# First layer of all tiles ahead of the feed-forward, low-rank term as a matrix per batch, gate once for all

## The chip, the cores and the metric

The kernel runs on one core of a Trainium2 chip. The metric is the device time of one execution in microseconds (us), as the median of several runs. The core has TensorE (matmul), VectorE, ScalarE and GpSimd, each with its own instruction queue in program order, and SyncE (SP), which here only issues transfers. Engines meet only at semaphores.

## The reference, cut to what matters

There are B = 32 batches of L = 128 tokens with D = 128 channels, R = 16 columns of `fside`, E = 4 experts and H = 512 hidden channels.

```python
# layer 0: linear + low-rank term made from fside, exact gelu, residual
z1 = einsum('bfi,bir->bfr', x, F) / 128          # F = fside[:, 0], 128 x 16 per batch
z  = einsum('bfr,bor->bfo', z1, F) / 16
x  = x + gelu_exact(x @ W.T + fc_bias + z + cond[:, None, :])

# layer 1: gate on means of token segments, top 2 of 4 experts, plus a shared one
gate_in = concat(mean(all), mean(head, proprio), mean(wrist, proprio))
logits  = (gate_in @ gate_w + gate_b) * (1 + scale) + shift   # scale, shift from silu(cond) @ time_w + time_b
w_be    = top-2 of softmax(logits), renormalised
for e in range(4):                                # expert 1 leaves out the wrist tokens, expert 2 the head tokens
    out += w_be[:, e] * mask[e] * (gelu_tanh(x @ ew1[e] + eb1[e]) @ ew2[e] + eb2[e])
x = x + out + gelu_tanh(x @ sw1 + sb1) @ sw2 + sb2
```

## The kernel before

Activations lie transposed, channels on the 128 partitions and tokens along the free dimension. A tile is NB = 4 batches, so TOK = 512 columns; there are NT = 8 tiles. Every product but transposes and small sums is done as three fp32r matmuls (`product3`, L541 to L546): each operand is split into a high half (rounded to fp32r) and a low half (the rest), and hi\*hi, lo\*hi and hi\*lo are added up in PSUM. So each weight and each activation needs a high and a low half, made by ScalarE, VectorE or GpSimd.

A feed-forward step is a pair (tile t, expert s), s = 0 being the shared one. `up(t, s)` on TensorE gives four chunks of 128 hidden channels in a ring of UP = 5 PSUM banks. `gelu` on ScalarE reads them into `h` (L468), for s = 0 a second time into `hs_hi` (L470). `split` on VectorE multiplies `h` by the routing weight into `hs_hi` (L864) and `hs_lo` (L872), four batches each; for expert 4 the high half is ScalarE's (`expert4_high`, L452), and the shared low half is GpSimd's (`shared_low`, L371). `down` on TensorE adds the second product of all five steps up in one bank. Experts 2 and 3 (s = 2, 3) work on 344 of the 512 columns. Then VectorE adds the residual (`outT`, L901), TensorE transposes, ScalarE copies, SP stores.

The loop runs over tiles, two in a pass. Inside the steps of tile t stands, in small pieces, the first layer of tile t + 1: transposing `x` (`xT`, L564), its two halves, the low-rank input product with `F` (`low_rank_in`), a mask to keep each batch to its own 16 rows (`z1_mask`, L754), the halves of `z1` and `fT` (`fT_low`, L762 and L764), `layer0` (L541 to L598) with five products, the exact gelu (`gelu0`, L437, with a table switch at L442), `residual0` (L771 to L775), the segment sums and the gate of four batches (`gate_in`, `gate_logits`, `gate_weights`, L782 to L838). Loads are issued by SP two tiles ahead. GpSimd adds the output biases into `x1` (L362). All order is written out by hand: each engine's program is a fixed list with semaphore waits.

Of the kernel before, what the change touches and what calls it, by code (L numbers as in the profile page):

```python
# [6 lines left out]
F32R = mybir.dt.float32r  # L19
# [5 lines left out]
def build(nc, x, fside, cond, W, fc_bias, gate_w, gate_b, time_w, time_b,  # L25
# [14 lines left out]

    NS = E + 1
    SPAN = [(0, L), (0, L), (0, HEAD + PROP), (HEAD, L), (0, L)]
    Z_SCALE = 1.0 / (D * R)
    ZR = NB * R
    BIAS_HI, BIAS_LO = ZR, ZR + 32
    UP = 5
    BANK_Y, BANK_OUT, BANK_L0 = 5, 6, 7


    GATE_LINKS = 14  # L50

    with ExitStack() as ctx:
# [8 lines left out]

        x_tok = sb("x_tok", [128, 2, NB, D])
        F_raw = sb("F_raw", [128, 2, 2, ZR])
        W_raw = sb("W_raw", [128, D])
        cond_raw = sb("cond_raw", [B, D])

        cond_rows = sb("cond_rows", [128, 2, D])
# [13 lines left out]
        batch_rows = sb("batch_rows", [128, NB])  # L81
        zmask_halves = sb("zmask_halves", [128, 2, NB])
        zmask = sb("zmask", [128, NB])
        before = sb("before", [128, NB, E, E])

        WT_hi = sb("WT_hi", [128, D], F32R)
        WT_lo = sb("WT_lo", [128, D], F32R)
# [40 lines left out]
        equal = sb("equal", [128, NB, E, E])
# [873 lines left out]
```

## Time and profile before

| | us |
|---|---|
| median of 3 runs | 275.53 |
| lowest, highest | 274.08, 276.33 |
| span of the profiled execution | 274.8 |
| busy: TensorE, VectorE, ScalarE, GpSimd | 243.5, 242.8, 190.5, 86.3 |
| one tile in the loop (151.0 to 181.8) | 30.8 |

The span is that of one execution under the profiler, from the first to the last instruction. Busy time is the time in which an engine has an instruction at work. Matmuls are pipelined: one is still in flight when the next two have started, so their price is the distance between starts, not their length.

### The profile page before, as it was taken

The numbers are of one execution on the slowest core, as the hardware profiler recorded it, in microseconds if no ns is written. First come the engines' busy times: TensorE is split into PE (matmuls) and PEld (weight loads), VectorE is DVE, ScalarE is ACT, GpSimd is POOL, SyncE is SP. The second block draws the span as 40 slices with busy tenths as digits, with TensorE's granted clock in tenths as the row PEclk, the third lists the DMA queues.
The fourth block names the chain that finished last, engine by engine and source line by source line (L and its number), as shares of the span: only waits on it lengthen the run. The fifth ranks groups of instructions, "written<-read, shape, count | busy, mean of one in ns | idle before, by whom it ended". The sixth has DMA issues, their size and how long they took to land.

```text
span 274.8 us, 4417 instructions
## 1 busy us (share of the span) xinstructions
PE 243.5 (89%) x1235; PEld 206.0 (75%) x1235; DVE 242.8 (88%) x582; ACT 190.5 (69%) x331; POOL 86.3 (31%) x99
## 2 busy tenths in 40 slices
PE   8849929999889988999889988999889988999995
PEld 8637818987678767987678767987678767988884
DVE  2995999989997999989998999989997999999863
ACT  3936823996489856896489846896489856895361
POOL 7449503063301513062301513062302523070200
PEclk9977977999999999999999999999999999999999
DMA  4950000002100030002000030002000010001001
GB/s 118 327 98 2 1 0 1 0 2 75 15 2 0 0 87 0 0 0 76 10 0 0 0 87 0 0 0 78 9 0 0 0 41 2 0 0 38 2 0 38
DMA packets 20340, 7.63 MB, mean 28 GB/s; under 512 B 10644, under 2 KB 19048, under 8 KB 20328
## 3 DMA queue, kind: packets, MB, share of 16 engines
q1 hardware_dynamic: 19309, 7.28, 10.4%
q10 hardware_dynamic: 859, 0.19, 0.3%
q8 instruction: 5, 0.08, 0.1%
q0 software_dynamic: 160, 0.02, 0.1%
q14 instruction: 7, 0.06, 0.1%
HBM read 5.39 MB, written 2.10 MB: 27 GB/s over the span
## 4 chain that ended last, share of the span: by engine, by line
DVE 45%; PE 36%; issue 15%; ACT 2%; DVEq 1%; POOL 0%; POOLq 0%
PE ps L541 12%; PE ps L546 11%; PE ps L542 11%; DVE hs_lo L872 11%; DVE hs_hi L864 6%; DVE fT_bias L762 4%; DVE equal L813 3%; DVE outT L901 2%; DVE W_lo L242 2%; DVE z L754 2%; DVE logit L804 2%; PE ps L557 2%; DVE F_hi L745 1%; ACT h L468 1%; DVE equal L815 1%
## 5 line engine op out<-in xcount | busy, mean ns | idle before, releaser
L468 ACT ACTIVATE h<-ps,b_col 128x512 f32<-128x512 f32 (+1 forms) x160 | 97.1, 632 | 53.0 <-PE ps L546 52.9
L541 PE MATMUL ps<-hs_hi,W_hi 128*128 128x512 f32 (+3 forms) x180 | 65.9, 366 | 17.2 <-DVE hs_lo L872 17.1
L872 DVE SCALAR_TENSOR_TENSOR hs_lo<-h,w_be,hs_hi 128x512 fp32r<-128x512 f32 (+1 forms) x128 | 76.3, 657 | 2.7 <-ACT hs_hi L452 2.7
L371 POOL TENSOR_TENSOR hs_lo<-h,hs_hi 128x512 fp32r<-128x512 f32 x32 | 40.4, 1294 | 91.9 <-ACT hs_hi L470 91.9
L542 PE MATMUL ps<-hs_hi,W_lo 128*128 128x512 f32 (+3 forms) x180 | 63.1, 351 | 0.0
L546 PE MATMUL ps<-hs_lo,W_hi 128*128 128x512 f32 (+3 forms) x180 | 63.1, 350 | 0.0
L541 PE MATMUL ps<-x_hi,W_hi 128*128 128x512 f32 (+1 forms) x160 | 59.5, 372 | 3.9 <-DVE x_hi L773 3.9
L546 PE MATMUL ps<-x_lo,W_hi 128*128 128x512 f32 (+1 forms) x160 | 59.3, 371 | 0.5 <-DVE x_lo L775 0.5
L542 PE MATMUL ps<-x_hi,W_lo 128*128 128x512 f32 (+1 forms) x160 | 59.2, 370 | 0.0
L541 PEld LDWEIGHTS ps<-hs_hi,W_hi 128*128 128x128 f32 x180 | 34.4, 191 | 26.0 <-DVE hs_lo L872 22.7
L864 DVE TENSOR_SCALAR hs_hi<-h,w_be 128x344 fp32r<-128x344 f32 (+1 forms) x97 | 43.1, 505 | 4.6 <-ACT h L468 3.5
L546 PEld LDWEIGHTS ps<-hs_lo,W_hi 128*128 128x128 f32 x180 | 34.3, 191 | 4.0
L542 PEld LDWEIGHTS ps<-hs_hi,W_lo 128*128 128x128 f32 x180 | 34.4, 191 | 3.3
L541 PEld LDWEIGHTS ps<-x_hi,W_hi 128*128 128x128 f32 x160 | 30.5, 191 | 8.1 <-issue 4.0
L546 PEld LDWEIGHTS ps<-x_lo,W_hi 128*128 128x128 f32 x160 | 30.7, 192 | 5.3 <-DVE x_lo L775 1.2
L542 PEld LDWEIGHTS ps<-x_hi,W_lo 128*128 128x128 f32 x160 | 30.6, 191 | 4.1
L470 ACT ACTIVATE hs_hi<-ps,b_col 128x512 fp32r<-128x512 f32 x32 | 22.2, 693 | 0.0
L354 POOL TENSOR_TENSOR z_lo<-z,z_hi 64x512 fp32r<-64x512 f32 x7 | 9.0, 1284 | 37.9 <-ACT z_hi L433 37.9
L452 ACT ACTIVATE hs_hi<-h,w_be 128x512 fp32r<-128x512 f32 x31 | 19.9, 711 | 0.4
L349 POOL TENSOR_TENSOR xT_lo<-x,xT_hi 128x512 fp32r<-128x512 f32 x7 | 9.7, 1387 | 23.3 <-ACT xT_hi L422 23.3
L362 POOL TENSOR_TENSOR x<-x,bias 128x168 f32<-128x168 f32 (+1 forms) x24 | 11.2, 491 | 8.4 <-DVE bias L849 8.4
L242 POOL TENSOR_TENSOR W_lo<-W_raw,W_hi 128x512 fp32r<-128x512 f32 x7 | 10.9, 1568 | 8.2 <-DVE W_hi L236 4.1
(134 smaller groups left out, 289.6 us busy)
## 6 DMA issues: line engine op xcount, KB each, us to landing
W_raw<-in_L_cond_ew SPq DMA_DIRECT2D x8, 256.0 KB, 4.6
out<-out_tok SPq DMA_DIRECT2D x7, 256.0 KB, 2.2
x_tok<-in_x SPq DMA_DIRECT2D x16, 84.0 KB
x_tok<-in_x SPq DMA_DIRECT2D x7, 88.0 KB
W_raw<-in_L_cond_sw SPq DMA_DIRECT2D x2, 256.0 KB, 4.0
F_raw<-in_fside_Bx1x1024x SPq DMA_DIRECT2D x15, 32.0 KB, 2.1
cond_rows<-in_cond SPq DMA_DIRECT2D x16, 2.0 KB
out<-out_tok SPq DMA_DIRECT2D x2, 128.0 KB, 1.8
```

The costliest lines, as they stand in the source:

```text
L242: eng.tensor_tensor(lo, raw, f32(hi), ALU.subtract).then_inc(w_lo_ok[n], 1)
L362: nc.gpsimd.tensor_tensor(xb[:, :, at:at + n], xb[:, :, at:at + n], bias2[:, i, :].unsqueeze(2).to_broadcast([128, NB, n]), ALU.add).then_ ...
L371: nc.gpsimd.tensor_tensor(hs_lo[:, hf, c, :], h[:, hf, c, :], f32(hs_hi[:, hf, c, :]), ALU.subtract).then_inc(shared_lo_ok, 1)
L452: nc.scalar.activation(hs_hi[:, hf, :, c], h[:, hf, :, c], ACT.Copy, scale=w_be[:, b, E - 1:E]).then_inc(hi4_ok, 1)
L468: ins = nc.scalar.activation(dst, up_bank(s, c), ACT.Gelu_apprx_tanh, bias=b1_col[:, s, c:c + 1])
L470: ins = nc.scalar.activation(hs_hi[:, hf, c, :], up_bank(s, c), ACT.Gelu_apprx_tanh, bias=b1_col[:, s, c:c + 1])
L541: nc.tensor.matmul(dst, w_hi, m_hi, start=start, stop=False)
L542: nc.tensor.matmul(dst, w_lo, m_hi, start=False, stop=False)
L546: return nc.tensor.matmul(dst, w_hi, m_lo, start=False, stop=stop)
L762: nc.vector.tensor_tensor(fT_bias[lo_rows, :], cond_rows[lo_rows, par, :], f32(fT_bias[lo_rows, :]), ALU.subtract).then_inc(fT_lo_ok, 1)
L864: nc.vector.tensor_scalar(hs_hi[:, hf, :, c], h[:, hf, :, c], w_be[:, b, s - 1:s], None, ALU.mult).then_inc(hi_ok, 1)
L872: nc.vector.scalar_tensor_tensor(hs_lo[:, hf, :, c], h[:, hf, :, c], w_be[:, b, s - 1:s], f32(hs_hi[:, hf, :, c]), ALU.mult, ALU.subtract) ...
```

## The change

Everything is unrolled in Python; there is no loop instruction left. The work is in three stages:

- **First layer of all tiles.** `x1` and its halves have room for all 8 tiles. The low-rank term is folded into the weight: per batch `F F^T` is made by one fp32 matmul from the transposed `F` (`matrices`), VectorE scales it and adds `W^T` (`matrix`, the tile `mat`), and one fp32 matmul per batch gives the layer (`layer0`). So no halves, no mask, no `z1`. `fc_bias + cond` is one bias column per batch (`bias0`), and `gelu0` is four ScalarE instructions of 128 columns a tile.
- **The gate once.** The segment sums are taken two tiles at a time, the gate of all 32 batches in one sequence. It stands between the splits of the first three steps.
- **The feed-forward as a list of 40 steps** (`STEPS`): (0,0), (1,0), then for each tile its experts 1 to 4 followed by the shared step of tile t + 2. TensorE does `up(k + 2)`, `down(k)`. `h` has three buffers. VectorE now makes the high half of expert 4 and the shared low half (two instructions of 1024 columns); GpSimd only adds the 24 bias pieces after the gate. All low halves of weights are VectorE's (`weight_low`), all high halves ScalarE's (`weight_high`).

Loads: `x` and `fside` come in four chunks of 1, 1, 2 and 4 tiles (`CHUNKS`), all issued at the start; `fside` is loaded once and not twice.

```diff
-    UP = 5
+    CHUNKS = [(0, 1), (1, 2), (2, 4), (4, 8)]
+    STEPS = [(0, 0), (1, 0)]
+    for t in range(NT):
+        STEPS += [(t, s) for s in range(1, NS)]
+        if t + 2 < NT:
+            STEPS.append((t + 2, 0))
+    RING = [0, 1, 4, 2, 3]
+    UP = len(RING)
...
+            load_x(0, SEGS[:2])
+            load_F(1)
+            load_x(1)
+            load_F(2)
+            load_x(2)
+            load_weight(0)
+            load_weight(1)
+            load_F(3)
+            load_x(3)
...
+            pool.wait_ge(bias2_ok, 1)
+            for t in range(NT):
+                xb = x1[:, t, :].rearrange("p (b l) -> p b l", l=L)
...
+            def gelu0(t):
+                act.wait_ge(y_ps, t + 1)
+                if t >= 2:
+                    act.wait_ge(x1_ok, t - 1)
+                for b in range(NB):
+                    ins = nc.scalar.activation(g0[:, t % 2, b * L:(b + 1) * L], psY0[t % 2][:, b * L:(b + 1) * L],
+                                               ACT.Gelu, bias=bias0[:, t * NB + b:t * NB + b + 1])
+                ins.then_inc(g0_ok, 1)
+            def gelu(k):
+                t, s = STEPS[k]
+                if k == 2:
+                    act.wait_ge(x1_ok, NT)
+                if k >= 3:
+                    act.wait_ge(lo_ok, parts_until(k - 3))
+                if s == 0 and k >= 2:
+                    act.wait_ge(down_ok, k - 1)
...
+            for t in range(NT):
+                if t + 2 < NT:
+                    xT_copy(t + 2)
+                    fT_copy(t + 2)
+                gelu0(t)
+                if t in (3, 4):
+                    weight_high(t - 3)
+            act.wait_ge(b1_in, 32)
+            weight_high(2)
+            gelu(0)
+            gate_tanh()
+            weight_high(3)
+            gelu(1)
+            for n in range(4, 2 * NS):
+                weight_high(n)
+            for k in range(2, K):
+                gelu(k)
+                t, s = STEPS[k - 3] if k >= 3 else (0, 0)
+                if s == NS - 1:
+                    out_copy(t)
...
+            def matrices(t):
+                pe.wait_ge(fT_ok, t + 1)
+                if t >= 2:
+                    pe.wait_ge(M_ok, t - 1)
+                for b in range(NB):
+                    last = nc.tensor.matmul(psM[t % 2][:, b * D:(b + 1) * D], fT[:, t % 2, b, :], fT[:, t % 2, b, :],
+                                            start=True, stop=True)
+                last.then_inc(M_ps, 1)
...
+            for t in range(NT):
+                if t + 1 < NT:
+                    matrices(t + 1)
+                if t + 2 < NT:
+                    xT(t + 2)
+                    transpose_F(t + 2)
+                layer0(t)
+                if t == 3:
+                    pe.wait_ge(bias_in, 16 * 3)
+                    pe.wait_ge(silu_ok, 1)
+                    nc.tensor.transpose(psEb2T, eb2_raw[:, :], ident[0:E, 0:E]).then_inc(eb2T_ps, 1)
+                if t == 4:
+                    pe.wait_ge(eb2T_read, NSEG)
+                    pe.wait_ge(mod_terms_ok, 1)
+                    nc.tensor.matmul(psMod, ones[:, :], mod_terms[:, :, :], start=True, stop=True
+                                     ).then_inc(mod_ps, 1)
+            up(0)
+            pe.wait_ge(mod_read, 1)
+            pe.wait_ge(gate_fold_ok, 1)
+            nc.tensor.matmul(psLogit, ones[:, :], gate_fold[:, :, :], start=True, stop=True).then_inc(logit_ps, 1)
+            up(1)
+            for k in range(K):
+                if k + 2 < K:
+                    up(k + 2)
+                down(k)
+                t, s = STEPS[k - 1] if k >= 1 else (0, 0)
+                if s == NS - 1:
...
+                    out_transpose(t)
...
+            for t in range(NT):
+                if t + 1 < NT:
+                    matrix(t + 1)
+                residual(t)
+                if t == 2:
+                    time_gate()
+                if t == 4:
+                    output_rows()
+                if t == 5:
+                    dve.wait_ge(bias_in, 16 * 3)
+                    modulation()
+                halves(t)
+                if t % 2 == 1:
+                    segment_sums(t - 1, t + 1)
+                if t in (4, 5):
+                    weight_low(t - 4)
+            gate_in()
+            weight_low(2)
+            split(0)
+            gate_logits()
+            weight_low(3)
+            split(1)
+            gate_weights()
+            split(2)
+            output_biases()
+            for n in range(4, 2 * NS):
+                weight_low(n)
+            for k in range(3, K):
+                t, s = STEPS[k - 2]
+                if s == NS - 1:
+                    out_sum(t)
+                split(k)
+            out_sum(NT - 1)
```

In `up(k)`, TensorE waits for `w_lo_ok` (the low half of its weight) for tile 0's steps, and for `h_ok` of the chunk that had the bank five chunks before. In `split(k)`, VectorE waits for `h_ok` of all four chunks and for `down(k - 2)`. `residual`, `halves` and `matrix` are the VectorE steps of one tile of the first layer, `eb2T_read` is counted by `output_rows`.

## Rows read from the trace of the kernel before

**Rows 1.** The page: busy times, chain that ended last, rate of transfers, stores.
```profile
PE 243.5 (89%) x1235; PEld 206.0 (75%) x1235; DVE 242.8 (88%) x582; ACT 190.5 (69%) x331; POOL 86.3 (31%) x99
GB/s 118 327 98 2 1 0 1 0 2 75 15 2 0 0 87 0 0 0 76 10 0 0 0 87 0 0 0 78 9 0 0 0 41 2 0 0 38 2 0 38
...
DVE 45%; PE 36%; issue 15%; ACT 2%; DVEq 1%; POOL 0%; POOLq 0%
...
out<-out_tok SPq DMA_DIRECT2D x7, 256.0 KB, 2.2
```

**Rows 2.** Stretches: length, busy (count) by engine, granted clock, DMA share, GB/s.
```profile
40.00:45.00 5.00, 4.58 (x12) 3.68 (x13) 4.83 (x12) 0.63 (x1) 2.61 (x4) 0.57 0.00 0
151.00:181.80 30.80, 28.13 (x140) 23.51 (x140) 28.50 (x70) 22.91 (x40) 8.82 (x10) 1.00 0.08 19
```

**Rows 3.** Groups by line and shape: count, busy us, mean ns, idle before.
```profile
L371 POOL TENSOR_TENSOR hs_lo<-h,hs_hi 128x512 fp32r<-128x512 f32 x32 | 40.4, 1294 | 91.9 <-ACT hs_hi L470 91.9
...
L442 ACT ACT_TABLE_LOAD x8 | 10.3, 1283 | 2.6 <-issue 2.5
```

**Rows 4.** Timeline of one tile in the loop: start, length, engine, line.
```profile
150.88 0.69 ACT L468 ACTIVATE h<-ps,b_col 128x512 f32<-128x512 f32 x1
151.04 0.40 PE L542 MATMUL ps<-hs_hi,W_lo 128*128 128x512 f32 x1
...
152.01 0.71 ACT L468 ACTIVATE h<-ps,b_col 128x512 f32<-128x512 f32 x1
...
152.91 0.40 PE L541 MATMUL ps<-x_hi,W_hi 128*128 128x512 f32 x1
...
155.41 0.39 PE L546 MATMUL ps<-x_lo,W_hi 128*128 128x512 f32 x1
...
159.03 2.59 DVE L864 TENSOR_SCALAR hs_hi<-h,w_be 128x512 fp32r<-128x512 f32 x4 [0.31 <-issue]
...
160.21 0.32 PE L541 MATMUL ps<-x_hi,W_hi 128*128 128x344 f32 x1
...
161.97 0.32 PE L546 MATMUL ps<-x_lo,W_hi 128*128 128x344 f32 x1
```

**Rows 5.** Timeline of the first 51 us, same columns.
```profile
1.07 3.36 PE L557 MATMUL ps<-ones 128*128 128x128 f32 x14 [1.07 <-POOL ones L316]
4.38 1.09 PE L564 MATMUL ps<-ident,x_tok 128*128 128x128 f32 x4
...
10.02 3.94 DVE L242 TENSOR_TENSOR W_lo<-W_raw,W_hi 128x512 fp32r<-128x512 f32 x2
...
27.02 1.72 PE L557 MATMUL ps<-ones 128*128 128x128 f32 x14
...
27.75 0.17 DVE L804 TENSOR_TENSOR logit<-logit,gate_add 128x16 f32<-128x16 f32 x1
...
28.49 1.13 ACT L415 ACTIVATE W_hi<-W_raw 128x512 fp32r<-128x512 f32 x1
28.58 0.60 PE L564 MATMUL ps<-ident,x_tok 128*128 128x128 f32 x4
...
29.16 1.08 DVE L242 TENSOR_TENSOR W_lo<-W_raw,W_hi 128x512 fp32r<-128x512 f32 x1
...
31.80 0.63 ACT L415 ACTIVATE W_hi<-W_raw 128x512 fp32r<-128x512 f32 x1
...
36.04 1.68 DVE L864 TENSOR_SCALAR hs_hi<-h,w_be 128x512 fp32r<-128x512 f32 x4
...
37.63 2.74 DVE L872 SCALAR_TENSOR_TENSOR hs_lo<-h,w_be,hs_hi 128x512 fp32r<-128x512 f32 x4
...
40.42 0.79 PE L541 MATMUL ps<-hs_hi,W_hi 128*128 128x512 f32 x1 [4.19 <-DVE hs_lo L872]
...
47.77 1.32 DVE L864 TENSOR_SCALAR hs_hi<-h,w_be 128x344 fp32r<-128x344 f32 x4 [0.38 <-ACT h L468]
...
49.01 2.03 DVE L872 SCALAR_TENSOR_TENSOR hs_lo<-h,w_be,hs_hi 128x344 fp32r<-128x344 f32 x4
```

More of the change, by code:

```diff
@@ L198, in build @@
+        psOut = ps[:, 7, :]
         block = ctx.enter_context(nc.Block())
@@ L201, in f32, with chunk_of @@
             return ap.bitcast(F32)
+        def chunk_of(t):
+            return next(c for c, (a, z) in enumerate(CHUNKS) if a <= t < z)
         def span(ap, s):
@@ L444, in expert4_high @@
-            def expert4_high(t, par, first=0):
-                act.wait_ge(w_ok, t + 1)
-                act.wait_ge(h_ok, CH * (NS * t + NS))
-                for b in range(first, NB):
-                    c = slice(b * L, (b + 1) * L)
-                    hf = half(par, NS - 1)
-                    nc.scalar.activation(hs_hi[:, hf, :, c], h[:, hf, :, c], ACT.Copy, scale=w_be[:, b, E - 1:E]
-                                         ).then_inc(hi4_ok, 1)
-            def gate_tanh(t):
-                act.wait_ge(logit_x_ok, t + 1)
-                nc.scalar.activation(tanh_g[:, :, :], logit_x[:, :, :], ACT.Tanh, scale=0.5).then_inc(tanh_g_ok, 1)
@@ L529, in _, with gate_tanh, out_copy @@
-            gelu(0, 0, 1)
-            weight_high(9)
-            with act.Fori(0, NT - 3, 2) as t:
-                tile(t, 0)
-                tile(t + 1, 1)
-            tile(NT - 2, 0)
-            tile(NT - 1, 1, last=True)
+            def gate_tanh():
+                act.wait_ge(logit_x_ok, 1)
+                nc.scalar.activation(tanh_g[:, :, :], logit_x[:, :, :], ACT.Tanh, scale=0.5).then_inc(tanh_g_ok, 1)
+            def out_copy(t):
+                act.wait_ge(out_ps, t + 1)
+                nc.scalar.activation(x_tok[:, t, :, :], psOut.rearrange("p (b d) -> p b d", d=D), ACT.Copy
+                                     ).then_inc(out_tok_ok, 1)
@@ new lines, in down @@
+            def down(k):
+                t, s = STEPS[k]
+                if t == 0:
+                    pe.wait_ge(w_lo_ok, 2 * s + 2)
+                if s == 0 and t >= 2:
+                    pe.wait_ge(outT_ok, NSEG * (t - 1))
+                elif s == 0 and t == 1:
+                    pe.wait_ge(M_ok, NT)
+                    pe.wait_ge(fT_ok, NT)
+                pe.wait_ge(lo_ok, parts_until(k))
+                for c in range(CH):
+                    last = product3(span(psY[t % 2], s), W2_hi[:, s, c, :], W2_lo[:, s, c, :],
+                                    span(hs_hi[:, k % 2, c, :], s), span(hs_lo[:, k % 2, c, :], s),
+                                    s == 0 and c == 0, s == NS - 1 and c == CH - 1)
+                last.then_inc(down_ok, 1)
@@ L970, in _ @@
[L970 to L977 removed]
+            dve.wait_ge(WT_ok, 1)
+            matrix(0)
+            dve.wait_ge(condT_ps, 1)
+            nc.vector.tensor_copy(condT[:, :], psCondT).then_inc(condT_ok, 1)
+            dve.wait_ge(fcb_in, 16)
```

913 lines of the change are left out of this document (305 added, 608 removed).

## The prediction

> **What bounds the kernel now.** I read four views. The page's engine totals and chain come first [rows 1]: TensorE 89% and VectorE 88% busy, the chain of work that ended last split between VectorE (45%), TensorE (36%) and 15% of waits without a named cause. The reader should see two engines taking turns. The table by stretches [rows 2] shows one tile of the loop: 30.8 us, TensorE busy 28.1 at the full clock, VectorE 28.5. The groups [rows 3] show who makes the shared low half today: GpSimd, 32 of 1294 ns. ScalarE scales the fourth expert's high half. The timelines [rows 4, 5] give unit prices, always from start to start, since matmul ends overlap.
>
> TensorE: eight steps from 151.04 to 152.91 are 0.234 us for a 512-column matmul of `down`; 11 steps from 152.91 to 155.41 are 0.227 in `up`; 11 from 160.21 to 161.97 are 0.160 at 344 columns [rows 4]. A 128-column plain fp32 matmul stands as two passes: (1.72 - 0.15)/13 = 0.12 a pass; a transpose is (0.60 - 0.2)/3 = 0.13 [rows 5]. So 60 products of `up` and 60 of `down` cost 36 x 0.227 + 36 x 0.234 + 48 x 0.160 = 24.3 us a tile, and four output transposes 0.5: 24.8. The other 6 us of today's 30.8 are first-layer work and waits.
>
> **The stream afterwards.** All first-layer, gate and GpSimd work leaves the loop. TensorE keeps 24.8 us a tile. VectorE takes over the fourth expert's high half and the shared low half. With GpSimd idle its prices are the free ones [rows 5]: four 512-column scalings 1.68 us (2.59 in a tile where GpSimd runs [rows 4]), four of the low half 2.74, at 344 columns 1.32 and 2.03. Experts: 2 x 4.4 + 2 x 3.35 = 15.5. The shared half, two of 1024 columns, is not shown; between the 1.08 of a strided 512-column subtraction [rows 5] and 1.3 (half of the 2.74 for 4 x 512), I take 1.16 each: 2.3. Output sum 0.8. Total 18.6 us, under 24.8. ScalarE: 0.57 us per 512-column gelu (two in 152.01 - 150.88 [rows 4]), 0.46 at 344: 16 x 0.57 + 8 x 0.46 + 0.5 = 13.3. TensorE should bound.
>
> But one stall is new. `gelu` of a shared step k now waits for `down` of k-2 (`down_ok`), since it writes `hs_hi[k % 2]`; `down(k-2)` comes behind `up(k)`. Queued behind that gelu is everything of ScalarE, and TensorE's next `up(k+1)` waits for its `h_ok` through the ring of five banks. Counted from the end of `down(k-2)`: the first shared chunk is released after 2 x 0.57 + 0.2 = 1.35, the third after 3.65. `up(k+1)` writes chunk 0 at once, may write chunk 1 at 1.35 and chunk 3 only at 3.65, where without waiting it would start at 3 x 0.68 = 2.05. The difference, 1.6, with the handovers 1.8, is lost once per shared step from tile 2 on, six times: 10.8 us. A tile then takes 24.8 + 1.8 = 26.6 against 30.8 now.
>
> **The opening.** Tile 0's `x` is there at 4.4 [rows 5]. TensorE does 8 transposes (cold, 0.22 each), W's, the first matrices (8 passes, 1.0), tile 1's transposes, then after ScalarE's two copies `matrices(1)`, tile 2's transposes and `layer0(0)`: 12.9. Four gelus, and `residual(0)` starts at 14.0. Each tile costs TensorE 16 x 0.12 + 8 x 0.13 = 3.0 us and VectorE 3.1: `matrix` 0.67 (a two-input product of 512 columns is 2.74/4 [rows 5]), residual 0.62 and low half 0.68 (the same kind, estimated), high half 0.48 (a scaling, 1.68/4, and its handover), sums 0.67 (estimate, three reduces for two tiles at 0.45). Up to `residual(7)` that is 7 x 3.1 = 21.8. VectorE also does `time_gate` 1.6, `output_rows` 0.5, `modulation` 1.4 and two low halves of weights, 1.1 + 0.65: 5.2 in all (small operations at 0.2 [rows 5], 128 columns at 0.3 to 0.45). The two queues also hold each other up. TensorE's `mod` matmul waits for `eb2T_read`, which VectorE gives after `residual(4)`; behind it stand `matrices(6)`, `xT(7)` and `layer0(5)`. It idles 3.7 us, VectorE then 3.4 before `residual(5)` and 1.3 before `residual(7)`: 4.7 on the path. 14.0 + 21.8 + 5.2 + 4.7 = 45.7. Loads I cost at nothing: `xT(4)`, the first to need the last chunk, stands at 16.8, and `x`, `fside` and two weights, 2.9 MB, take 9 us at the 327 GB/s of the page's best slice [rows 1]. Without that cover each us later is a us of the path.
>
> **The gate, once.** It must end before `split(2)`, the first with a routing weight, and VectorE, ScalarE take turns. From 45.7: `gelu0(7)` is just done; `weight_high(2)` 1.1 (1.13 and 0.63 for the two kinds [rows 5]), table load 1.3 [rows 3], eight gelus 4.6: 52.7. `split(0)` 2.3: 55.0. Four operations up to `logit_x` 1.2, tanh 0.25, `weight_high(3)` 0.6, eight gelus: 61.7. Then ScalarE has `weight_high(4)` to (9), 3 x 1.08 + 3 x 0.56 = 4.9, in front of `gelu(2)`: 66.7, which is done at 69.0. `split(2)` 4.4: 73.5. Output biases 1.6 and `weight_low(4)` 1.1: 76.2. Only then may `up(3)` start. In these 31 us TensorE did three `up` and one `down`; it stands for 10.6 us before `up(3)`. In the kernel before, the wait for the first routed half was 4.2 us, ending at 40.42 [rows 5].
>
> After such an idle the clock is low: the stretch 40 to 45 us shows a granted 0.57 [rows 2], so 1.2 GHz up to about 44.3, roughly 4 us after the restart. I take 5 us, 2.3 lost.
>
> **The sum.** 76.3; eight tiles 198.2, less three `up` (8.2) and one `down` (2.8): 187.2; cold clock 2.3; six stalls 10.8; `down(39)` waits for its own split, which nothing follows, 2.9; output sum, copy, handovers and the store's 2.2 [rows 1]: 4.2. Together 283.7 us of span. The profiled execution of before is 274.8, its median 275.5, so I add 0.7: **284 us**, 3% slower. Put as a difference: 4.2 x 7 = 29 us gained in the stream, about 36 lost ahead of it, the rest at the end (the halves of the last tile are gone).
>
> Unknown prices. GpSimd adds all 24 bias pieces (11 us) just as VectorE makes `weight_low(4)` to (9). A low half stands at 2.0 under such contention and 1.08 without [rows 5]: 0.9 before `up(3)`, the others hidden behind `down(1)` and `up(4)`. From 0 to 2; I take 0. Tanh after Gelu early on may need its table: of the 1.28 us load [rows 3] two would cost ScalarE 2.6 and the path 0.8; I take none. The Trainium skill, "ScalarE: Activation LUTs", Table sets, lists tanh with exp and sigmoid and Gelu in another set: by it the sum is 284.5; no row here shows the pair.
>
> **Rivals.**
> *Cold opening.* TensorE has pauses in the opening; at 1.2 GHz a tile costs it 16 x 0.24 + 8 x 0.22 = 5.6 us, it bounds, and `residual(7)` moves by 11: 295. For it: 0.24 a pass is what the first 14 take [rows 5]. Against it: two thirds of its work there are plain matmuls, and it is busy 3.0 of 3.1 us. The Trainium skill, "TensorE: Matmul & The Clock Gate", Part 4, says that transposes do not count as activity; by that rule this case is likelier, and a third of the opening's work is transposes. Chance 0.1.
> *Not slower: ScalarE's shared gelu holds nobody up.* It would, if its start came 1.8 us earlier against `up(k+1)`, that is if `down(k-2)` of 344 columns ended before `up(k)` was through. The stream then takes 24.8 a tile: 284 - 10.8 = 273, within 1% or just past it. It decides from 6 us saved. Against it is the order of the queue: `down(k-2)` stands behind `up(k)`. Chance 0.1.
> *VectorE or ScalarE bound in the stream.* If the scalings stay near the 2.59 of today [rows 4] or a gelu takes 0.69 (its own length [rows 4]) from start to start, 288 to 291. Chance 0.15.
> *Shorter opening.* If the `mod` hold-up does not form and TensorE stays warm: 284 - 4.7 - 1.3 = 278. Chance 0.1. With the stall gone as well it would be below 272. All remaining chance, 0.55, is my forecast's.
>
> Here 1% is about what a measurement can tell from no change: 272.8 to 278.3 is the same. Slower 0.75 (forecast nearly whole, cold opening, other engines), same 0.17 (no stall, short opening), faster 0.08 (both). Range 275 to 293: it leaves out the colder half of the cold case and most of the no-stall case.
>
> **What would show it.** A start of `up(3)` near 76 with TensorE idle some 10 us before; a tile of 26.6 us with TensorE at full clock; a wait of about 1.8 us inside the `up` behind each shared step, released by ScalarE; VectorE near 70% and ScalarE near 50% in the loop. If `up(3)` starts before 68, or the loop's tile is under 25.3, I am wrong.

## The result

The changed kernel takes 287.5 us (median of 4 runs, 286.5 to 289.3) against 274.9 (274.1 to 276.3) of the kernel before: ratio 1.044, 95% interval 1.039 to 1.049, so 4.4% slower. The profiled execution has a span of 287.6 us, against 274.8 before. Ratios here and below leave disturbed executions out, so a ratio is not always the quotient of the two medians.

The page of the changed kernel answers to [rows 1]: busy times, then two of the rows by 40 slices (7.2 us each; tenths of busy time, tenths of full clock), then the chain that ended last.

```profile
span 287.6 us, 3352 instructions
PE 248.7 (86%) x1205; PEld 209.1 (73%) x1205; DVE 194.9 (68%) x395; ACT 142.9 (50%) x264; POOL 19.8 (7%) x39
...
PE   7889678554199999989998999899899989999964
...
PEclk9899755968579999999999999999999999999989
...
PE 67%; ACT 14%; DVE 8%; SPq 4%; issue 3%; DMA 2%; DVEq 0%; ACTq 0%
```

VectorE fell from 88% to 68% and GpSimd from 31% to 7%. The chain now belongs to TensorE for 67%, with ScalarE second. The slices show where TensorE rests (the 5, 5, 4, 1 of slices 8 to 11, about 50 to 79 us) and where its clock was down (slices 5 to 7 and 9 to 12).

**The loop.** The table by stretches, as [rows 2], with the stretch's length, busy time and count by engine, granted clock, DMA share and GB/s:

```profile
103.00:129.70 26.70, 25.57 (x125) 21.43 (x125) 18.19 (x37) 14.20 (x26) 0.00 (x0) 1.00 0.04 11
129.70:156.30 26.60, 25.53 (x124) 21.38 (x124) 18.19 (x37) 14.11 (x26) 0.00 (x0) 1.00 0.04 11
```

The chain passes the same matmul at 103.03, 129.68, 156.33, 182.99, 209.64 and 236.29 us: a tile is 26.65 us, against 30.80 before. VectorE needs 18.2 of it and ScalarE 14.2.

**The opening and the gate stage.** The residuals of tiles 0, 1, 5 and 7 (L533), what TensorE waited for in between, and the restart, from the timeline (start, length, engine, line, count, idle time before it and who ended it), which answers to [rows 5]:

```profile
11.30 0.82 PE L383 MATMUL ps<-ident,x_tok 128*128 128x128 f32 x4 [0.88 <-DMA x_tok<-in_x]
...
12.76 1.92 PE L409 MATMUL ps<-x,h 128*128 128x128 f32 x8
...
15.88 0.69 DVE L533 TENSOR_TENSOR x<-x,h 128x512 f32<-128x512 f32 x1 [4.74 <-ACT h L304]
...
19.09 0.69 DVE L533 TENSOR_TENSOR x<-x,h 128x512 f32<-128x512 f32 x1 [0.73 <-ACT h L304]
...
20.02 0.66 PE L383 MATMUL ps<-ident,x_tok 128*128 128x128 f32 x4 [1.06 <-DMA x_tok<-in_x]
...
31.38 0.70 PE L489 MATMUL ps<-mod_terms,ones 128*128 128x256 f32 x2 [3.26 <-DVE eb2T L608]
...
38.80 0.69 DVE L533 TENSOR_TENSOR x<-x,h 128x512 f32<-128x512 f32 x1 [4.08 <-ACT h L304]
...
47.73 0.69 DVE L533 TENSOR_TENSOR x<-x,h 128x512 f32<-128x512 f32 x1 [1.58 <-ACT h L304]
...
54.81 2.36 DVE L561 TENSOR_TENSOR hs_lo<-h,hs_hi 128x1024 fp32r<-128x1024 f32 x2 [1.74 <-ACT hs_hi L321]
...
58.38 0.31 ACT L327 ACTIVATE tanh_g<-logit_x 128x128 f32<-128x128 f32 x1 [3.60 <-DVE logit_x L638]
...
63.67 4.81 ACT L286 ACTIVATE W_hi<-W_raw 128x512 fp32r<-128x512 f32 x6
...
76.60 1.89 DVE L551 TENSOR_TENSOR W_lo<-W_raw,W_hi 128x512 fp32r<-128x512 f32 x2
...
77.72 0.66 PE L370 MATMUL ps<-x_hi,W_hi 128*128 128x344 f32 x1 [9.52 <-DVE W_lo L551]
```

`residual(7)` starts at 47.7 and `up(3)` at 77.7, after TensorE stood for 9.5 us. Before, TensorE's wait for the first routed half ended at 40.42 [rows 5]. So that restart comes 37.3 us later, and what is behind it takes 209.9 us where it took 234.4: 24.5 us shorter. The difference, 12.8 us, is the whole difference of the two spans.

### The profile page after: what moved, and what is told of

It reads as the page before. It is cut to its first block, busy times and chain, and to the rows that moved or that the text cites. A ratio compares the mean times of both kernels' runs of the same rounds, so it can differ in the third digit from the quotient of the medians.

```text
span 287.6 us, 3352 instructions
## 1 busy us (share of the span) xinstructions
PE 248.7 (86%) x1205; PEld 209.1 (73%) x1205; DVE 194.9 (68%) x395; ACT 142.9 (50%) x264; POOL 19.8 (7%) x39
## 4 chain that ended last, share of the span: by engine, by line
PE 67%; ACT 14%; DVE 8%; SPq 4%; issue 3%; DMA 2%; DVEq 0%; ACTq 0%
PE ps L370 20%; PE ps L372 20%; PE ps L371 19%; ACT h L318 6%; ACT hs_hi L321 4%; SPq L198 3%; PE ps L409 3%; DVE hs_lo L572 3%; DMA x_tok<-in_x 2%; ACT W_hi L286 2%; PE ps L399 2%; DVE hs_hi L567 2%; PE ps L458 1%; DVE hs_lo L561 1%; PE ps L383 1%
## 5 line engine op out<-in xcount | busy, mean ns | idle before, releaser
L572 DVE SCALAR_TENSOR_TENSOR hs_lo<-h,w_be,hs_hi 128x512 fp32r<-128x512 f32 (+1 forms) x128 | 77.3, 665 | 0.0
L567 DVE TENSOR_SCALAR hs_hi<-h,w_be 128x512 fp32r<-128x512 f32 (+1 forms) x128 | 49.4, 448 | 26.3 <-PE ps L372 25.0
L370 PE MATMUL ps<-hs_hi,W_hi 128*128 128x512 f32 (+1 forms) x160 | 60.2, 376 | 2.5 <-DVE hs_lo L572 2.5
L372 PE MATMUL ps<-hs_lo,W_hi 128*128 128x512 f32 (+1 forms) x160 | 59.5, 372 | 0.0
L371 PE MATMUL ps<-hs_hi,W_lo 128*128 128x512 f32 (+1 forms) x160 | 59.3, 371 | 0.0
L561 DVE TENSOR_TENSOR hs_lo<-h,hs_hi 128x1024 fp32r<-128x1024 f32 x16 | 18.9, 1221 | 33.2 <-ACT hs_hi L321 33.2
L271 POOL TENSOR_TENSOR x<-x,bias 128x168 f32<-128x168 f32 (+1 forms) x24 | 15.7, 691 | 71.6 <-DVE bias L675 71.6
L331 ACT ACTIVATE x_tok<-ps 128x512 f32<-128x512 f32 x8 | 4.8, 599 | 30.3 <-PE ps L458 30.3
L409 PE MATMUL ps<-x,h 128*128 128x128 f32 x64 | 12.2, 353 | 2.9 <-issue 2.9
L304 ACT ACTIVATE h<-ps,bias 128x128 f32<-128x128 f32 x32 | 9.1, 367 | 9.7 <-PE ps L409 9.7
L409 PEld LDWEIGHTS ps<-x,h 128*128 128x128 f32 x64 | 11.1, 261 | 3.6 <-issue 3.4
```

The source lines that it names most:

```text
L271: nc.gpsimd.tensor_tensor(xb[:, :, at:at + n], xb[:, :, at:at + n], bias2[:, i, t * NB:(t + 1) * NB].unsqueeze(2).to_broadcast([128, NB, n ...
L304: ins = nc.scalar.activation(g0[:, t % 2, b * L:(b + 1) * L], psY0[t % 2][:, b * L:(b + 1) * L], ACT.Gelu, bias=bias0[:, t * NB + b:t * NB ...
L370: nc.tensor.matmul(dst, w_hi, m_hi, start=start, stop=False)
L371: nc.tensor.matmul(dst, w_lo, m_hi, start=False, stop=False)
L372: return nc.tensor.matmul(dst, w_hi, m_lo, start=False, stop=stop)
L409: last = nc.tensor.matmul(psY0[t % 2][:, b * L:(b + 1) * L], mat[:, t % 2, b, :], x1[:, t, b * L:(b + 1) * L], start=True, stop=True)
```

## The experiments

The kernels below are the changed kernel with the edit shown; nothing is left out of the computation in any. "Idle matmuls" are 128-column fp32 products of ones into a PSUM bank that nothing reads before it is overwritten; they only keep TensorE busy. The times, and three numbers from each one's profile that tell the runs apart (starts in us, and the time from `up(3)` to the end):

| kernel | median us | ratio to before | residual(7) | up(3) | up(3) to end |
|---|---|---|---|---|---|
| changed kernel | 287.5 | 1.044 | 47.7 | 77.7 | 209.9 |
| e_swap | 278.1 | 1.011 | 47.6 | 77.5 | 196.9 |
| e_modlate | 284.7 | 1.031 | 45.0 | 75.0 | 208.0 |
| e_warmmod | 286.5 | 1.041 | 45.9 | 75.9 | 207.9 |
| e_warmopen2 | 290.9 | 1.045 | 50.7 | 80.6 | 210.0 |
| e_warmgate | 288.2 | 1.044 | 50.2 | 80.2 | 205.9 |
| e_gatefirst2 | 285.9 | 1.036 | 48.5 | 74.7 | 210.2 |
| e_high | 288.7 | 1.046 | 49.9 | 77.3 | 208.0 |
| e_pool | 281.2 | 1.021 | 49.2 | 67.7 | 209.8 |

Each ratio's interval is 0.4 to 0.8% to either side. The kernel before took 274.9 us beside the changed kernel and 276.1 to 276.5 beside the others, so ratios compare whole times better than medians do: 1% is 2.8 us. The opening also differs from execution to execution: in the profiles of the eight kernels other than e_warmopen2, none of whose edits acts before it, `residual(1)` starts anywhere from 19.1 to 22.8 us. So stages are compared below from one point of the profile to the next; each is read in one execution.

### 1. The stall in the loop

`down(k)` is put ahead of `up(k+2)` where that one is of a shared step, so that the shared gelu finds `down_ok` done:

```diff
+                early = k + 2 < K and STEPS[k + 2][1] == 0
+                if early:
+                    down(k)
                 ...
-                down(k)
+                if not early:
+                    down(k)
```

> TensorE's queue only: where the step after next is a shared one, down(k) is issued before up(k + 2), so ScalarE's shared gelu can start 1.9 us earlier against the following up. My theory (the wait for down(k-2) behind up(k) holds ScalarE and through the ring TensorE): the 1.8 us wait inside six ups is gone, a tile takes 24.8 us and not 26.65, the whole 10 to 11 us less (about 277). Rival (ScalarE's double gelu, 1.15 us a chunk against 0.68 of TensorE, fills the ring whatever the order): the wait stays above 1 us a tile and the gain is under 4 us.

Measured: 278.1 us, ratio 1.011 (1.002 to 1.019). The stretches of e_swap:

```profile
100.00:124.80 24.80, 24.80 (x125) 21.66 (x125) 18.20 (x37) 14.18 (x26) 0.00 (x0) 1.00 0.04 12
124.80:149.60 24.80, 24.80 (x125) 21.64 (x124) 18.21 (x37) 14.18 (x26) 0.00 (x0) 1.00 0.04 11
```

The tile is 24.80 us with TensorE busy all of it; the work on the other engines is the same to 0.1 us. In the changed kernel the four chunks of the `up` behind a shared step start so:

```profile
99.15 0.39 PE L370 MATMUL ps<-x_hi,W_hi 128*128 128x512 f32 x1
...
100.71 0.50 PE L370 MATMUL ps<-x_hi,W_hi 128*128 128x512 f32 x1 [0.71 <-ACT hs_hi L321]
...
101.87 0.50 PE L370 MATMUL ps<-x_hi,W_hi 128*128 128x512 f32 x1 [0.20 <-ACT hs_hi L321]
...
103.03 0.50 PE L370 MATMUL ps<-x_hi,W_hi 128*128 128x512 f32 x1 [0.19 <-ACT hs_hi L321]
```

Three chunks take 3.88 us from start to start where 3 x 0.70, e_swap's distance, would do: 1.78 lost, in the three places where ScalarE must free a bank. (The idle times in brackets add up to less, 1.10, because a matmul that nothing presses on from behind is drawn longer.) The page of waits sums this kind over the span (total, times, longest); the changed kernel:

```profile
PE ps L370 <- ACT hs_hi L321: 10.8, 19, 4.2
```

and e_swap:

```profile
PE ps L370 <- ACT hs_hi L321: 4.2, 1, 4.2
```

The one that stays is the first shared gelu's, behind the table load, and has nothing to do with `down_ok`. Eighteen are gone, three for each of six steps. So the stall is this wait and nothing else: 26.65 - 24.80 = 1.85 us a tile, 11.1 for the six. The span behind `up(3)` fell by 13.0; most of the other 1.9 is the clock, which was down in the last `down` in the profile of the one and not of the other, and for a shorter time behind the restart (section 3). The medians differ by 9.4 (9.2 by the ratios), a little under the 10 to 11 expected; the spans differ by more, as e_swap's profiled execution was its fastest and the changed kernel's its slowest.

### 2. The hold-up by the modulation's matrix

e_modlate moves TensorE's `psMod` product (and VectorE's `modulation()`) behind the last first layer:

```diff
-                if t == 4:
-                    pe.wait_ge(eb2T_read, NSEG)
-                    pe.wait_ge(mod_terms_ok, 1)
-                    nc.tensor.matmul(psMod, ...)
+            pe.wait_ge(eb2T_read, NSEG)
+            pe.wait_ge(mod_terms_ok, 1)
+            nc.tensor.matmul(psMod, ...)
```

> The one matmul psMod moved from behind layer0(4) to behind layer0(7), and VectorE's modulation behind gate_in. My theory (this matmul waits for VectorE's eb2T, everything behind it in TensorE's queue waits too, and the clock falls after it): TensorE's pause of 3.3 us at 28 us is gone, no stretch at 1.2 GHz between 31 and 49 us, residual(7) 4 to 8 us earlier, the whole 4 to 7 us less. Rival (the opening is bound by VectorE's own queue, the pause only changes its place): under 2 us.

e_warmmod leaves the wait and fills it with 13 idle matmuls:

```diff
                 if t == 4:
+                    pe.wait_ge(xT_ok, 6)
+                    for _ in range(13):
+                        nc.tensor.matmul(ps[:, 1, 0:128], ones[:, :], ones[:, :], start=True, stop=True)
                     pe.wait_ge(eb2T_read, NSEG)
```

> The order is left as it is, but TensorE fills the pause ahead of psMod with 13 idle fp32 matmuls (3.2 us), so that only the clock differs. If the low clock from 31 to 49 us follows from that pause, the clock stays full, the first-layer work of the last tiles (8 us busy at 1.2 GHz) takes half, and up(3) starts 3 to 5 us earlier. Rival (transposes and 16-row matmuls keep the clock low in any case, or VectorE bounds this stretch): under 1.5 us.

Measured: 284.7 (ratio 1.031, 1.024 to 1.038) and 286.5 (1.041, 1.033 to 1.049). From `residual(1)` to `residual(7)` the changed kernel takes 28.6 us (19.09 to 47.73 above), e_warmmod 25.7 and e_modlate 22.2:

```profile
22.76 0.69 DVE L531 TENSOR_TENSOR x<-x,h 128x512 f32<-128x512 f32 x1 [3.12 <-ACT h L304]
...
45.00 0.69 DVE L531 TENSOR_TENSOR x<-x,h 128x512 f32<-128x512 f32 x1 [1.57 <-ACT h L304]
```

The difference is 6.4 us. Of these, 1.4 are `modulation()` itself, four operations of VectorE that e_modlate makes only behind `residual(7)`; there they do not lengthen the path, since `up(3)` stands 30.0 us behind `residual(7)` in both. By e_warmmod, 3.0 are not the wait but the clock after it; 2.0 are left for the wait. Of the 6.4, e_modlate's profile keeps 2.7 at `residual(7)`, since its `residual(1)` happened to come 3.7 us later, and its whole time is 3.6 us less by the ratios, under the 4 to 7 expected. The stretches behind the wait, changed kernel first, with the last but two column the granted clock:

```profile
30.00:46.00 16.00, 11.75 (x49) 10.17 (x50) 11.14 (x26) 3.46 (x10) 0.00 (x0) 0.57 0.00 1
```

and e_warmmod:

```profile
30.00:38.00 8.00, 7.59 (x58) 6.44 (x56) 5.80 (x15) 2.72 (x8) 0.00 (x0) 1.00 0.00 1
38.00:46.00 8.00, 3.33 (x12) 3.06 (x13) 6.18 (x15) 2.38 (x9) 0.00 (x0) 0.57 0.01 3
```

With the wait filled the clock holds to 38 us; then a second idle time of 4.7 us comes, in which TensorE waits for VectorE's matrix of tile 7 (it starts at 41.9, behind the modulation, the sums and a low half), and it falls after all. That, and a `residual(1)` 1.2 us later, is why e_warmmod keeps only a part of the gain: 1.8 us at `residual(7)` and at `up(3)`, more than its rival's 1.5 and less than its theory's 3 to 5. In e_modlate too the clock did not stay up, as had been expected: behind its waits of 1.49 and 3.08 us it was granted 0.50 from 40 to 44 us.

### 3. The clock in the opening and at the restart

e_warmopen2 adds 9 idle matmuls where TensorE waits in the first 16 us:

```diff
+            keep_busy(2)
             matrices(0)
             ...
+            keep_busy(3)
             ...
+                if t == 0:
+                    keep_busy(4)
```

> The changed kernel with idle fp32 matmuls added where TensorE waits in the opening: 2 ahead of matrices(0), 3 behind the transpose of F for batch 1, 4 ahead of the transposes of tile 2. Nothing is left out and nothing else moves. Theory: the opening's spread from profile to profile (residual(1) between 16.9 and 22.8 us) is TensorE's clock at its lower level after its waits; with the waits filled residual(1) stands at 18 us or earlier, residual(7) at 46 or earlier, and the whole time is 284 to 286 us. Rival: the opening waits for loads and for VectorE, the clock costs nothing there; residual(1) stays at 19 us or later, and the time is within 1 us of the changed kernel's.

Measured: ratio 1.045 (1.040 to 1.050), no gain. The profiled execution was the slowest of its four (292.3 us, the fastest 287.2), so it shows what can happen in this opening and not what each execution does. In it `residual(1)` came at 17.4, as the theory had it, but `residual(7)` at 50.7. The timeline and the stretches say why:

```profile
17.43 0.69 DVE L537 TENSOR_TENSOR x<-x,h 128x512 f32<-128x512 f32 x1 [0.52 <-ACT h L304]
...
20.39 0.66 PE L383 MATMUL ps<-ident,x_tok 128*128 128x128 f32 x4 [3.09 <-DMA x_tok<-in_x]
```

```profile
20.00:24.00 4.00, 3.61 (x21) 3.31 (x22) 1.15 (x3) 2.00 (x6) 0.00 (x0) 0.69 1.00 352
24.00:28.00 4.00, 4.00 (x19) 3.47 (x19) 3.50 (x11) 1.39 (x3) 0.00 (x0) 0.50 0.36 130
```

TensorE arrives earlier and waits 3.09 us for the last chunk of `x` (1.06 in the changed kernel), and behind that longer wait its clock is at the lower level from 21 to about 28 us. The last chunk came when it came in the others (the transposes behind this wait start at 20.0 to 20.9 us in each of the five profiles that have it). So the theory was right that the clock makes `residual(1)` late (with the waits filled it is granted 1.00 from 8 to 16 us, and 0.50 in e_modlate, whose `residual(1)` was the latest), and wrong about its worth: the load comes next, and haste only moves the idle time.

e_warmgate adds 38 idle matmuls before `up(3)` and 12 before the last `down`:

```diff
+                if k == 1:
+                    pe.wait_ge(fT_ok, NT)
+                    pe.wait_ge(M_ok, NT)
+                    for _ in range(38):
+                        nc.tensor.matmul(ps[:, 6, 0:128], ones[:, :], ones[:, :], start=True, stop=True)
+                if k == K - 1:
+                    pe.wait_ge(outT_ok, NSEG * (NT - 1))
+                    for _ in range(12):
+                        nc.tensor.matmul(ps[:, 5, 0:128], ones[:, :], ones[:, :], start=True, stop=True)
```

> Only idle fp32 matmuls are added on TensorE: 38 (9.3 us) in the wait ahead of up(3) and 12 (3 us) in the wait ahead of the last down. My theory (each of the two waits drops the clock, and what follows runs at 1.2 GHz for about 5 and 3 us): up(3), down(1) and the last down at full clock, 2 to 4 us less. Rival (the slow start is hidden, because TensorE would only wait longer for split(2) to split(5)): only the 1.7 us of the last down.

Measured: 288.2, ratio 1.044 (1.039 to 1.048), no different from the changed kernel as a whole time. The stretches after the restart, changed kernel:

```profile
76.00:80.00 4.00, 2.28 (x8) 2.28 (x9) 3.96 (x6) 0.70 (x2) 3.23 (x4) 0.50 0.00 0
80.00:82.00 2.00, 2.00 (x8) 1.90 (x7) 2.00 (x3) 1.38 (x3) 2.00 (x2) 0.50 0.00 0
82.00:84.00 2.00, 2.00 (x7) 1.57 (x7) 0.59 (x1) 0.12 (x1) 2.00 (x5) 0.67 0.00 0
84.00:86.00 2.00, 2.00 (x13) 1.79 (x12) 0.70 (x2) 0.24 (x1) 2.00 (x6) 1.00 0.00 0
```

and e_warmgate:

```profile
80.00:82.00 2.00, 1.82 (x11) 1.82 (x12) 2.00 (x3) 0.97 (x3) 2.00 (x3) 1.00 0.00 0
```

The clock stays up, and from `up(3)` to the end the kernel takes 205.9 us, 4.0 less than the changed kernel. Where `up(4)` starts, 24 matmuls behind the restart, separates the two parts. The changed kernel is there at 85.02 us (restart at 77.72), e_warmgate here:

```profile
80.18 0.43 PE L370 MATMUL ps<-x_hi,W_hi 128*128 128x344 f32 x1 [1.33 <-DVE W_lo L560]
...
84.97 0.32 PE L370 MATMUL ps<-x_hi,W_hi 128*128 128x344 f32 x1
```

These 24 take 7.30 us and 4.79: the restart's clock costs 2.5. The other 1.5 are nearly all the last `down`'s, and an execution may get them without the edit. The last `down` waits 2.54 us in all the other kernels of the table; behind it the clock had fallen in the profiles of the changed kernel, e_gatefirst2, e_warmopen2 and e_pool, and had not in those of e_modlate, e_high, e_warmmod and e_swap. First the changed kernel's row, its 512-column matmul at 0.80 us, and then e_swap's, at 0.50:

```profile
278.26 0.80 PE L370 MATMUL ps<-hs_hi,W_hi 128*128 128x512 f32 x1 [2.54 <-DVE hs_lo L572]
```

```profile
266.49 0.50 PE L370 MATMUL ps<-hs_hi,W_hi 128*128 128x512 f32 x1 [2.54 <-DVE hs_lo L576]
```

The first seven matmuls of the last `down` take 3.1 us from start to start in the one and 1.7 in the other. So the last `down`'s clock is 1.4 us that an execution may or may not pay. The restart's is paid in more or less every one: up to `up(4)` the other kernels whose TensorE idles there take 6.2 to 7.5 us. The whole time of e_warmgate does not confirm these 4 us: its opening was 2.5 us later in the profiled execution, and the median gained nothing. Whether the opening's spread hid them stays open.

### 4. What the gate stage consists of

e_gatefirst2 puts the four operations up to `logit_x` ahead of `split(0)`, and the routing weights ahead of `split(1)`:

```diff
-            split(0)
             gate_logits()
+            split(0)
             ...
-            split(1)
             gate_weights()
+            split(1)
```

> The changed kernel with two groups of instructions moved on VectorE in the gate stage: gate_logits stands ahead of split_group(0), and gate_weights ahead of split_group(1). Nothing else moves. Theory: the order on VectorE is a part of the 30 us between residual(7) and up(3); ScalarE waits 3.60 us for logit_x before tanh in the changed kernel, and that wait falls below 1 us. up(3) then stands 26 to 28 us behind residual(7) (30.0 in the changed kernel), and the whole time is 2 to 4 us less: 284 to 286 us. Rival: the stage is bound by the sum of VectorE's work (splits, folds, low weights), whatever its order; up(3) stays 29 us or more behind residual(7) and the time is within 1 us of the changed kernel's.

Measured: 285.9, ratio 1.036 (1.031 to 1.041). Tanh starts at 55.4 without a wait and the stage is 26.2 us instead of 30.0. The order of two groups on VectorE was worth 3.8 us of the path. The theory's number for the stage holds; the whole time moved by 1.6 us by the medians and by 2.1 by the ratios, at the lower end of its 2 to 4.

e_high lets ScalarE make the high halves of weights 2 to 9 in the opening, out of the way of its gelus:

```diff
+                if t == 5:
+                    for n in (2, 3, 4, 5):
+                        weight_high(n)
+                if t == 6:
+                    for n in (6, 7, 8, 9):
+                        weight_high(n)
             ...
-            weight_high(2)
             ...
-            weight_high(3)
             ...
-            for n in range(4, 2 * NS):
-                weight_high(n)
```

> ScalarE's high halves of weights 2 to 9 are made in the opening (four behind gelu0(5), four behind gelu0(6)) and not between the gelus of the gate stage. My theory (ScalarE's queue is the gate stage's path: 1.1 + 0.6 + 4.9 us of weight halves stand in it): up(3) starts 5 to 6.5 us earlier, the whole 5 to 6.5 us less. Rival (the halves delay gelu0(6) and (7) by as much as they free later, or VectorE takes over as the path): under 3 us.

Measured: 288.7, ratio 1.046 (1.041 to 1.052): nothing gained. I expected ScalarE's 6.6 us of weight work to be the path, and of it 2.6 came off the stage (27.4 instead of 30.0). In the profile a `residual(7)` 2.2 us later took that back, and the edit isn't what made it late: `residual(1)`, before which it does nothing, was 2.6 later already, and from there to `residual(7)` the two kernels take 28.2 and 28.6. Why the four executions together show no gain stays open. The timeline of e_high shows who took over the stage:

```profile
49.90 0.69 DVE L535 TENSOR_TENSOR x<-x,h 128x512 f32<-128x512 f32 x1 [1.57 <-ACT h L304]
...
66.93 0.22 DVE L656 TENSOR_SCALAR denom<-tanh_g 128x128 f32<-128x128 f32 x1
...
70.41 1.68 DVE L569 TENSOR_SCALAR hs_hi<-h,w_be 128x512 fp32r<-128x512 f32 x4
```

In the changed kernel `split(2)` starts at 70.87, 23.1 us behind `residual(7)` and after 1.28 us of waiting for ScalarE's gelu; here at 70.41, 20.5 behind it, right behind `w_be` and without any wait. So VectorE's own row comes next, 2.6 us behind ScalarE's, and that is all that an edit of ScalarE alone can give. VectorE's sum over the stage says the same: busy 25.1 of the 30 us in the changed kernel.

e_pool gives GpSimd, idle until 76 us, the low halves of weights 4 to 9, on top of e_high:

```diff
+            for n in range(4, 2 * NS):
+                pool.wait_ge(w_hi_ok, n + 1)
+                raw, hi, lo = weight(n)
+                nc.gpsimd.tensor_tensor(lo, raw, f32(hi), ALU.subtract).then_inc(w_lo2_ok, 1)
             ...
-            for n in range(4, 2 * NS):
-                weight_low(n)
```

> The high halves early as before, and the low halves of weights 4 to 9 made by GpSimd, so that VectorE goes from the output biases straight to split(3). up(3) no longer waits for weight_low(4) behind split(2), so it starts right behind down(0), near 66 us and not 77; TensorE does up(3), down(1), up(4), 6.6 us of work, in the time in which it stood still. My theory (VectorE's and ScalarE's order around the gate is what TensorE waits for): 6 to 9 us less than the changed kernel. Rival (down(2) must wait for split(2) at 73 to 75 us anyway, and GpSimd's 1.3 to 1.5 us per weight slows VectorE's scalings): under 3 us.

Measured: 281.2, ratio 1.021 (1.017 to 1.025), 7.4 us less than e_high and 6.3 less than the changed kernel, of the 6 to 9 expected. `up(3)` comes 18.5 us behind `residual(7)`: it no longer stands behind the routed halves at all, since it needs only weights. What that costs shows in e_pool's timeline, VectorE's rows first and then GpSimd's, which is busy from 41.7 to 52:

```profile
41.08 0.43 DVE L543 CAST x_hi<-x 128x512 fp32r<-128x512 f32 x1
...
45.89 1.69 DVE L543 CAST x_hi<-x 128x512 fp32r<-128x512 f32 x1
...
49.19 2.07 DVE L539 TENSOR_TENSOR x<-x,h 128x512 f32<-128x512 f32 x1
```

```profile
41.70 9.02 POOL L270 TENSOR_TENSOR W_lo<-W_raw,W_hi 128x512 fp32r<-128x512 f32 x5 [36.53 <-ACT W_hi L290]
```

The same conversion takes 0.43 us alone and 1.69 beside GpSimd, a residual 0.69 and 2.07. The Trainium skill, "SBUF — State Buffer", section SBUF: two separate sides, says that the two engines share one port pair as an exclusive lock, which the loser waits for in full; the trace fits that (1.69 - 0.43 = 1.26 and 2.07 - 0.69 = 1.38 us, each less than one of GpSimd's operations, which last 1.50 to 2.05).

### 5. The parts together

Three kernels put together what helped. e_all: e_modlate, e_high, e_pool and e_swap.

> Four edits together: down ahead of up for shared steps, psMod late, high halves early, low halves 4 to 9 on GpSimd. Added up from their places: 10 + 5 + 2.6 + 6, some 22 to 25 us less than the changed kernel: 262 to 266, faster than the kernel before by 3 to 5%. If they overlap (the opening's gain waits again at the gate stage) 268 to 272.

Measured: 268.7, ratio 0.971 (0.967 to 0.975): the gains did not add up to the 262 to 266 of the theory, it is the overlapping case. e_all2 adds the order of e_gatefirst2 and five chunks of `x` with the first weights loaded behind them:

```diff
-    CHUNKS = [(0, 1), (1, 2), (2, 4), (4, 8)]
+    CHUNKS = [(0, 1), (1, 2), (2, 3), (3, 4), (4, 8)]
```

> As the one before, and two more: x in five chunks (tiles 2 and 3 apart) ahead of the shared weights, and VectorE's gate_logits ahead of split(0) and gate_weights ahead of split(1), so that ScalarE gets logit_x while it is still in gelu(0). My theory: the wait of ScalarE for logit_x (3.6 us) goes, split(2) ends 3 to 4 us earlier, the loads give up to 2: 257 to 262. Rival (the gate's own VectorE work, 9 us, is the path in either order): within 1 us of the one before.

Measured: 265.7, ratio 0.965 (0.959 to 0.970), which misses the theory's 257 to 262 and is 2 to 3 us under e_all, more than the rival's 1. `residual(7)` came at 42.9, `up(3)` at 62.1. e_all4 makes the modulation's product behind `layer0(6)`, with 10 idle matmuls in its wait and others in the opening and before the last `down`:

> All that helped, in one kernel: down(k) ahead of the shared up(k+2), weights 2 to 9's high halves made during the opening, low halves 4 to 9 by GpSimd, weight loads behind the x loads, gate_logits and gate_weights ahead of the splits, the modulation's matrix made behind layer0(6) with 10 idle matmuls in its wait, idle matmuls in the opening and before the last down. Theory: the wait for the modulation's matrix (4.87 us in the last such kernel) and the clock in the opening are what is left; the time is 258 to 263 us against 265.7 of that kernel and 275 to 276 of the kernel before. Rival: TensorE has other work to wait for there (VectorE's, which GpSimd slows), and the time is 265 us within 1.

Measured: 264.0 (261.4 to 268.2), ratio 0.953 (0.949 to 0.956). Four of its six executions lie at 261.4 to 264.4, at the upper end of the theory's 258 to 263 and past it; the rival had 264 to 266. The profile is of one of the other two, at 267.0 us, so its times are on the long side. It shows the wait that the rival named:

```profile
52.01 0.77 PE L509 MATMUL ps<-gate_fold,ones 128*128 128x128 f32 x2 [7.20 <-DVE gate_fold L652]
```

TensorE now waits 7.2 us for VectorE, which GpSimd slows (a 128-column sum of the modulation takes 1.25 us beside it and 0.29 in the changed kernel), and runs the eleven matmuls behind it at the lower clock. It is 4.7% faster than the kernel before. So the change's plan can win, and order and placement were what made it lose. Whether edits of this kind would also speed up the kernel before was not tried.

## Why the prediction was right, and where it was not

- *The stream, 26.6 a tile.* Measured 26.65, with 24.80 when the stall is taken away (the prediction: 24.8 and 1.8). All three unit prices of matmuls held, and so did the cause: one edit in the order of `down` removed 1.85 us. VectorE's 18.6 was 18.2 (the two 1024-column low halves lasted 2.36 together, taken as 2.3), ScalarE's 13.3 was 14.2.
- *The opening, `residual(7)` at 45.7.* It was 47.7. Three terms were off. `residual(0)`, forecast at 14.0, came at 15.9: the step "Loads I cost at nothing" failed, since chunks of `x` came later than the first needs of them (waits of 0.88 and 1.06 us). The forecast took 327 GB/s; from 8 to 20 us the loads moved 133 to 189. And the clock, still full while TensorE waited, fell about 0.4 us after the first of these waits had ended (1.00 from 10.4 to 11.3 us, 0.85 from 11.3 to 11.8, 0.50 behind), so the eight passes at 12.76 took 1.92 us and not 1.06. The hold-up of 4.7 by `mod` was 5.7 in VectorE's waits (4.08 and 1.58); it formed where it was forecast, from the wait that was named. What made it longer is the clock, which the forecast kept at full: 0.57 over 30 to 46 us. The rest of the stage was 0.9 shorter than forecast.
- *The cold opening, a rival at 0.1.* It came true in part. The clock was at its lower level from about 12 to 15 us and from 32 to 49, but not throughout, and VectorE's work covered a part of it: 3 us of the path, not 11. The reason given against it, "it is busy 3.0 of 3.1 us", did not hold: a single wait of 3.26 us was enough, behind which the clock fell within 1 us, and the busy engine stayed slow for long.
- *The gate stage, 30.6 us.* It was 30.0, with the operations in the order of the working and, counted from `residual(7)`, nearly at its times (tanh at 58.4, `split(2)` at 70.9). But e_high shows that the working's path, which went through ScalarE's weights, had a second one only 2.6 us behind it, VectorE's row of work. So taking 6.6 us of work off ScalarE alone was worth 2.6 us of the stage, and no gain shows in the whole time. The sum was right and said too little of what the stage hangs on.
- *The cold restart, 2.3.* The lower level lasted from 77.7 to about 83.3 us, 5.6 us; against e_warmgate it cost 2.5.
- *The end.* The wait before the last `down` was 2.5 (2.9 forecast). That it may let the clock fall was not forecast: in the profiled execution the first seven matmuls took 3.1 us from start to start and not 1.7, so 1.4 more. The very end was forecast at 4.2 and took 5.1 (from 282.5 to 287.6 us).
- *The sum.* 283.7 of span forecast, 287.6 measured: +1.4 up to `up(3)`, +0.2 for the restart, +1.4 for the clock in the last `down`, -0.4 for the wait before it, +0.9 at the very end, and 0.4 in the stream and small terms. The largest mis-sized thing is TensorE's clock after a wait: 3 us of the opening, of which shorter terms gave some back, and 1.4 at the last `down`. That the total lies this near owes something to such cancelling; the two largest terms, the stream and the gate stage, were right one by one.
- *Unknown prices.* GpSimd's contention: the six low halves took 5.99 us from 76.60 on, where 3 x 1.06 + 3 x 0.68 = 5.2 was the free price, so 0.8, and 0.06 of it before `up(3)`. Taking 0 was right, as GpSimd lost more (24 pieces of 0.69 us mean where the shortest is 0.46). The tanh table: none of the tanhs was preceded by a load of its own.

## What to carry over

Work moved out of a loop is paid ahead of it, one engine after the other: cost that stage by the engine that has the longest row of work there, and ask for each instruction whether it must stand before the restart. Where a wait on an older step is added, look at which side of the newer step's work that step stands; swapping the two was worth 1.85 us a tile here, beside the 4.15 that the whole change had gained. And where a forecast lets TensorE stand, price the matmuls behind the gap at both levels of the clock: here the same gap of 2.5 us was followed by either.

## What the hardware showed that was not expected

**A busy TensorE that stayed slow.** In the changed kernel:

```profile
32.00:40.00 8.00, 8.00 (x35) 7.02 (x35) 3.48 (x6) 2.32 (x6) 0.00 (x0) 0.51 0.00 1
```

TensorE is busy all 8 us with transposes, 16-row products and 128-column fp32 products, and the granted clock is 0.51 (1.2 GHz). In 12 to 16 us it was back at 2.4 GHz after some 3 us of the same kind of work. The Trainium skill, "TensorE: Matmul & The Clock Gate", Part 4: PE-mode transpose, says that transposes do not count as activity for the clock; that fits the long stretch and leaves the short one unexplained. No run here separates the two kinds of work.

**Contention of VectorE and GpSimd is no constant.** A VectorE conversion of 512 columns went from 0.43 to 1.69 us beside GpSimd's 512-column subtractions, while beside GpSimd's pieces of 168 and 176 columns the low halves of the weights went from 1.06 to at most 1.31.

**The same wait, two clocks.** A gap of 2.54 us before the last `down` was followed by the full clock in four profiles of the table and by the half one in four, with the same work ahead of it. Behind the wait of 4.2 us for the first shared gelu the clock fell in both, but not at the same moment: the first matmul behind it takes 0.79 us in the changed kernel and 0.50 in e_warmmod, where the next chunk's, 1.15 us later, is slow:

```profile
58.59 0.50 PE L370 MATMUL ps<-x_hi,W_hi 128*128 128x512 f32 x1 [4.21 <-ACT hs_hi L321]
...
59.74 0.79 PE L370 MATMUL ps<-x_hi,W_hi 128*128 128x512 f32 x1 [0.19 <-ACT hs_hi L321]
```

So the clock can also fall while the engine is already at work again. What decides stays open.

**A DMA issue can take 4.8 us.** The last three issues of `x` chunks took 5.80 us of the queue's time in the changed kernel, one of them 4.77. They are of the last chunk, the one that TensorE waited for at 20.02, 7.1 us after the last of them. Whether the long issue or the transfers made it late is not separated, and the chunk waited for at 11.30 had been issued before:

```profile
7.55 5.80 SPq L198 DMA_DIRECT2D x_tok<-in_x  x3
```
